# A recurrent block with an FP4 feed-forward gate: the unread identity products of the first chunk are taken out of TensorE's program

## The reference

```python
xn = layernorm(x)
# recurrent branch
x1 = causal_dwconv(rmsnorm(xn)) + xn          # 3 taps, then a 256 x 256 product
x2 = min_gru(rmsnorm(x1)) + x1                # gate and hidden: 256 x 512, then a scan over the tokens
s  = gelu(rmsnorm(x2) @ w1 + b1) @ w2 + b2 + x2   # 256 x 1024 and 1024 x 256
# gate branch, all operands rounded to FP4 in blocks of 16
h  = silu(fp4(xn) @ fp4(w_gate)) * (fp4(xn) @ fp4(w_up))   # 256 x 704, twice
g  = silu(fp4(h) @ fp4(w_down))                            # 704 x 256
out = x + s * g
```

## Time and profile before

| | us |
|---|---|
| median of 3 runs | 1067.97 |
| lowest and highest run | 1066.93, 1068.56 |
| the profiled execution's own time | 1067.32 |
| its span, from first to last instruction | 1065.5 |
| PE busy | 1048.0 (98%) |
| VectorE (DVE) busy | 976.0 (92%) |
| ScalarE (ACT) busy | 627.4 (59%) |
| GpSimd (POOL) busy | 117.5 (11%) |

### The profile page before, as it was taken

How to read it: one execution, slowest core, us unless ns; L and a number is a source line. 1 busy time by engine, 2 the same in 40 slices (tenths; PEclk the granted TensorE clock), 3 DMA queues, 4 the chain that set the end, 5 groups by cost and what they waited for, 6 DMA issues and landing times.

```text
span 1065.5 us, 18539 instructions
## 1 busy us (share of the span) xinstructions
PE 1048.0 (98%) x6924; PEld 970.0 (91%) x6924; DVE 976.0 (92%) x1883; ACT 627.4 (59%) x1010; POOL 117.5 (11%) x116
## 2 busy tenths in 40 slices
PE   7999999999999999999999999999999999999998
PEld 6788989999898999989999898999989899998998
DVE  7789999999999999999999999999999999999886
ACT  5675364574846557484565837456474655748452
POOL 1010102011020200102020010201102020010100
PEclk9999999999999999999999999999999999999999
DMA  7000001010010100001010010101001010100101
GB/s 252 1 20 2 1 21 41 21 40 2 22 40 21 41 20 19 23 21 41 21 41 21 1 41 21 41 21 41 14 8 40 21 41 21 39 3 1 41 1 60
DMA packets 29367, 31.47 MB, mean 30 GB/s; under 512 B 1120, under 2 KB 28512, under 8 KB 29280
## 3 DMA queue, kind: packets, MB, share of 16 engines
q1 hardware_dynamic: 28448, 29.43, 9.0%
q10 hardware_dynamic: 832, 0.87, 0.3%
HBM read 21.90 MB, written 8.39 MB: 28 GB/s over the span
## 4 chain that ended last, share of the span: by engine, by line
PE 67%; DVE 26%; ACT 3%; issue 3%; DMA 1%; POOL 0%; ACTq 0%; DVEq 0%
PE gu_ps L1065 35%; PE w_ps L1065 18%; DVE xs L575 3%; PE w_ps L1137 3%; DVE cand L573 2%; DVE cand L570 2%; DVE xs_lo L564 2%; DVE act_lo L527 2%; DVE q_y L411 2%; DVE hqt_lo L534 1%; DVE q_amax L399 1%; DVE hq L425 1%; ACT hqt_hi L858 1%; DVE hid L511 1%; PE gu_ps L1077 1%
## 5 line engine op out<-in xcount | busy, mean ns | idle before, releaser
L1065 PE MATMUL gu_ps<-gu_hi,xq_hi 128*128 128x352 f32 x512 | 167.8, 328 | 0.2 <-ACT act L888 0.2
L1065 PE MATMUL gu_ps<-gu_lo,xq_hi 128*128 128x352 f32 x512 | 165.7, 324 | 0.0
L1065 PE MATMUL gu_ps<-gu_hi,xq_lo 128*128 128x352 f32 x512 | 165.4, 323 | 0.0
L1065 PE MATMUL w_ps<-w_hi,act_hi 128*128 128x256 f32 x480 | 138.8, 289 | 0.8 <-DVE act_lo L527 0.8
L1065 PE MATMUL w_ps<-w_hi,act_lo 128*128 128x256 f32 x480 | 135.1, 282 | 0.0
L1065 PE MATMUL w_ps<-w_lo,act_hi 128*128 128x256 f32 x480 | 135.1, 281 | 0.0
L1065 PE MATMUL gu_ps<-xs_hi,w_hi 128*128 128x512 f32 x256 | 101.3, 396 | 0.0
L1065 PE MATMUL gu_ps<-xs_hi,w_lo 128*128 128x512 f32 x256 | 101.0, 394 | 0.0
L1065 PE MATMUL gu_ps<-xs_lo,w_hi 128*128 128x512 f32 x256 | 100.9, 394 | 0.0
L1065 PEld LDWEIGHTS gu_ps<-gu_hi,xq_hi 128*128 128x128 f32 x512 | 96.2, 188 | 0.5 <-issue 0.4
L1065 PEld LDWEIGHTS gu_ps<-gu_lo,xq_hi 128*128 128x128 f32 x512 | 96.3, 188 | 0.0
(11 more groups left out here) (156 smaller groups left out, 2710.0 us busy)
## 6 DMA issues: line engine op xcount, KB each, us to landing
x_in<-x_dram SPq DMA_DIRECT2D x16, 512.0 KB, 4.0
x_res<-x_dram SPq DMA_DIRECT2D x16, 512.0 KB, 4.8
out_dram<-o SPq DMA_DIRECT2D x15, 512.0 KB, 3.2
act<-w_t_dram SPq DMA_DIRECT2D x1, 1024.0 KB, 11.9
w_f<-w_t_dram SPq DMA_DIRECT2D x1, 1024.0 KB, 14.4
w_f<-w_down_dram SPq DMA_DIRECT2D x1, 704.0 KB, 9.9
hid<-w_gate_dram SPq DMA_DIRECT2D x1, 640.0 KB, 6.4
hid<-w_up_dram SPq DMA_DIRECT2D x1, 640.0 KB, 9.5
```

The costliest lines, as they stand in the source:

```text
L1065: done = M.matmul(psum, l, r, start=first and i == 0, stop=last and i == len(terms) - 1)
```

## The change

The function `keep_busy` and its six calls in `first` are taken out. Everything else stands as it was: the waits, the order of all other work on every engine, and all DMAs.

```diff
-            def keep_busy(n, bank):
-
-                for _ in range(n):
-                    M.matmul(bank[:, 0:P], ident[:], ident[:], start=True, stop=True)
...
             def first():
                 pe.wait_ge(ld_const, 32)
-                keep_busy(24, gu_ps[:, 0, 0, :])
                 front_xc(0)
-                keep_busy(14, gu_ps[:, 0, 0, :])
                 remainder(0, None)
                 remainder(1, None)
                 pe.wait_ge(pwlo_ready, 1)
                 pointwise(0)
                 front_xq(0)
                 weight(0)
-                keep_busy(9, gu_ps[:, 0, 0, :])
                 sum_squares(0, w_ps[:, 0, :], (x1_ready, KD))
-                keep_busy(10, gu_ps[:, 0, 0, :])
                 spread_scale(0, w_ps[:, 1, :], (x1_ready, KD))
...
                 for i in (4, 5):
                     remainder(i, (rest_ready, i - 1))
-                keep_busy(16, gu_ps[:, 1, 0, :])
                 sum_squares(1, gu_ps[:, 0, 0, :], (coef_ready, 1))
...
                 for i in (8, 9):
                     remainder(i, (rest_ready, i - 1))
-                keep_busy(4, gu_ps[:, 0, 0, :])
                 pe.wait_ge(rest_ready, 3 * KD)
                 ff1(0, (0, 1))
```

## The result

The changed kernel took 1069.97 us (median of 20 runs, 1068.61 to 1071.54) against 1067.95 us before (median of 20, 1066.69 to 1069.04). The ratio is 1.002 with a 95% interval of 1.0013 to 1.0027: 2.0 us slower, where +2.8 had been forecast. The profiled execution took 1069.18 us.

What follows compares the result with a forecast made beforehand. PE, busy 1048.0 of 1065.5 us, was taken to bound the kernel, so early losses last to the end. The terms +2.35 - 0.32 + 2.4 - 0.88 - 0.72 = +2.8 us on 1067.97 gave 1070.8 us, range 1066.6 to 1073.8.

Steps and rivals of the forecast that it cites:

- B: The forecast itself: beside the cold start, the clock falls once more, before `spread_scale(0)`; 1070.8 us, chance 0.37.
- First stretch: From the transposes of `xc` to the end of `pointwise(0)`: cold start, 5.2 us of work at half rate, +2.35 us.
- 9 products: Identity products behind `weight(0)`; without them `sum_squares(0)` starts earlier, -0.32 us.
- The fall before `spread_scale(0)`: PE nearly idle for 4.5 us behind `weight(0)`, so the clock falls; 5.2 us at half rate follow, +2.4 us.
- 16 products: Identity products before `sum_squares(1)`; without them its transposes start at 48.58 us, -0.88 us.
- 4 products: Identity products before `ff1`; without them it starts as soon as `xs_lo` is there, -0.72 us.
- Third idle stretch: PE idle for 2.7 us before `sum_squares(1)`; the clock holds, 0 us, or +2.6 us if it falls.
- Rival C: The clock falls before `sum_squares(1)` too: +5.4 us, 1073.4 us, chance 0.07.
- A: Only the cold start costs; transposes behind `weight(0)` keep the clock at 2.4 GHz: +0.4 us, 1068.4 us, chance 0.36.
- D: The clock rises before it matters, at `remainder(0)`; only the gains remain: -1.92 us, 1066.1 us, chance 0.12.
- E: Stretches of transposes let the clock fall or keep it from rising, up to `pointwise(0)` and behind: +5.8 us, 1073.8 us, chance 0.08.

Runs made afterwards that it cites:

- the transposes: As the run that decides against E: kernel before with all 77 identity products replaced by 154 transposes of the identity; 1067.93 against 1067.84 us, ratio 1.0.

## Why the prediction was right, and which terms were off

The mechanism held: the products that nobody reads keep TensorE's clock, and without them two stretches of chunk 0 run at half rate, while three small waits get shorter. The sign, the range (1066.6 to 1073.8) and the likeliest case (B, one fall more) fit the time. Step by step, with the working in the prediction:

- First stretch: +2.35 predicted. `pointwise(0)` ended 1.83 us later in the profile, but the whole execution had started earlier: `xc` was transposed at 13.07 and not at 13.68. Against that clock it is 1.83 + 0.61 = +2.44. The rise, 5.4 us after the remainders began, was that of the row used. It isn't always: it took 3.1 and 3.4 us in two other profiles, and by the same measure the first stretch lost 1.3 and 1.5 us there. Over its runs the kernel without 24 and 14 lost 2.0 us. That the execution had started earlier shows in ScalarE too, whose `xc` (L785) began at 11.23 against 11.84 us.
- 9 products: -0.32 predicted; `a` is 0.26 us shorter where the start is warm. The size came near by luck: the hand-over from VectorE took 0.05 us and not the 0.2 put in, so the transposes start 0.48 us earlier, and 0.22 go back because they start behind a wait (0.67 us against 0.45). In the changed kernel `a` is 0.45 us shorter. The other 0.2 is slack that the prediction missed: it put `sum_squares(0)` on ScalarE's squares, but with a warm start VectorE was still at its own queue when they were done, and only in the changed kernel did it wait for them, 2.15 us.
- The fall before `spread_scale(0)`: it came, as put, in both profiles of the changed kernel, and none of its 30 runs is without a low stretch. The size was off: +2.4 predicted, +1.35 measured. The low stretch lasted 3.4 us (33.1 to 36.5), not 5.2, and half of that is 1.7. About 0.3 us of it went where the chain of before held two short delays: 0.15 in the second pair of float32 instructions (1.01 us there, 0.86 elsewhere) and 0.14 in the first 12 gru matmuls (2.93 there, 2.79 in the changed kernel). That gives 1.4. The size taken from the start, 5.2 us, did not carry over: eight of the nine profiled falls lasted 3.4 us, the ninth 6.8.
- 16 products: -0.88 predicted, -0.85 to -0.87 measured in `c`, in every profile without them.
- 4 products: -0.72 predicted, and with all that `d` holds -0.20 measured. The step of the argument that failed is that a queue of matmuls which starts behind a wait takes as long as one behind other work. `ff1` paid 0.24 us for it and `sum_squares(1)` 0.22 (0.66 against 0.44 us).
- Third idle stretch: 0 predicted. That held in the first profile and not in general: `sum_squares(1)` was followed by 1.2 GHz in all three profiles whose clock had not fallen before it, and in the second profile of the changed kernel the fall came 1 us behind it. By the mean clocks, 8 of the 30 runs of the changed kernel had a second low stretch or a doubled one. Rival C, at 0.07, deserved more.
- From 60 us on nothing changed: `pointwise(1)` starts 37.69 us after the first 12 matmuls of `ff1` end, and 37.65 before; from the end of those 12 the span goes on for 1006.5 us, and 1006.6 before.

The sum of the measured terms of the first profile is 2.44 - 0.45 + 1.35 - 0.85 - 0.20 = +2.3 us. That profile's span is 1.6 us longer, to which the 0.6 of its earlier start belongs, 2.2 in all, and the medians give +2.0. The forecast +2.8 came from a fall costed 1 us too high and gains 0.4 us too high, which partly cancel: that it lies within 1 us is in part luck. Of the rivals, A is out by the profiles and the mean clocks (no run of the changed kernel is without a fall), D by the kernel without 24 and 14, whose every run is slower than before's median, and E by the transposes.

Left open: why an idle stretch of 2.4 to 2.7 us is followed by a fall in one run and not in another. The mean clocks show how often (4 of 11 for 2.4 us alone, 20 of 33 for 2.7), and nothing on record shows what decides it: where the stretch lies in time and what went before were not told apart. Open too is the 1 us that the kernel without 16 spends outside its span.

## What to carry to other kernels

Filler work on TensorE has two separate effects: it keeps the clock, and it delays the next real step where it runs over the moment at which that step's operand lands. Size each piece to end just ahead of that moment, read from the timeline of the other engines. By the medians, taking all of it out cost 2.0 us here, trimming it won 1.3. And read the durations of one repeated instruction as well as the granted clock, since the first low stretch stood only in the durations. Where an effect comes in some executions only, one profile can't tell its price: read the mean clock of all runs beside it.

## What the runs showed of the hardware that had not been expected

- A single idle stretch of 2.4 us on TensorE, with work on both sides, was followed by a stretch at 1.2 GHz in 4 of 11 runs, one of 2.7 us in 20 of 33, and the pair of 1.55 and 2.4 us with four transposes between came with one in 11 of 11. Idle 1.2 us before the gate weights, in every profile, was followed by none.
- A low stretch lasted 3.4 us in eight of nine profiled falls and 6.8 in the ninth, by the granted clock.
- The column of the granted clock reads 1.00 in the low stretch at the start of each execution (421 ns against 275 ns for one matmul) and 0.50 in the later ones.
- A fall of 3.4 us cost 1.3 to 1.6 us, at or under the half of its length that half rate on the chain would cost: two short delays of the chain before took up 0.3 us of it behind `spread_scale(0)`.
- Float32 transposes of 128 columns, back to back, lifted and held the clock as other float32 matmuls of their shape did (421 to 273 ns, against 421 to 275).
